# Four-layer graph network kernel: longer row and one-hot rings in passes 2 and 3, more lead, later closing steps

## The chip, the cores and the metric

One core of one Trainium2 chip runs the whole program. The metric is the device time of one execution in microseconds (us), the median of the runs. Engines are named as in the profile: PE (TensorE matmuls), PEld (its weight loads), DVE (VectorE), ACT (ScalarE), POOL (GpSimd) and SP (SyncE, which only issues DMAs here).

## The reference, cut to what matters

There are 6250 nodes with 256 features and 106250 edges, sorted by destination. Four layers follow each other, each with a residual and a layer norm. The third entry below (a two-step GCN) is what passes 2 and 3 of the kernel compute.

```python
edge_index = jnp.stack([src, dst])
x = _layernorm(x + _L0_gnn_ref(x, edge_index, ...))       # attention, gathers of x
x = _layernorm(x + _L1_gnn_ref(x, L1_gnn_W, edge_index))  # pass 1
# pass 2 is the first gcn_layer, pass 3 the second
def gcn_layer(x, row, col, w, W, b, n):
    x = x @ W
    deg = jax.ops.segment_sum(w, col, num_segments=n)
    dinv = jnp.where(deg > 0, jax.lax.rsqrt(deg), 0)
    norm = dinv[row] * w * dinv[col]
    return jax.ops.segment_sum(norm[:, None] * x[row], col, num_segments=n) + b
h = relu(gcn_layer(X, row, col, w, W1, b1, n)); h = relu(gcn_layer(h, row, col, w, W2, b2, n))
x = _layernorm(x + h)
x = _layernorm(x + _L3_gnn_ref(x, L3_gnn_W, edge_index))  # last pass
```

## The kernel before, in words

The nodes are cut into 49 blocks of 128. A segment sum into one block is done in one of two ways. In passes 2 and 3 the first 27 blocks are summed **by gathers**: 18 chunks of up to 128 edges each, so that a pass has 27 x 18 = 486 chunks. The other 22 blocks are summed **densely**: a count-and-weight matrix of the block (built in pass 1, kept in DRAM as `AW`) is loaded in pieces `aw` and multiplied with all rows of the layer (`H` in pass 2, `H4` in pass 3), 49 units of a block, 1078 units in a pass. `dense_of` (line 271) spreads the units evenly over the chunks, between two and three to a chunk.

One chunk of pass 2 or 3, numbered m over the passes and k within one, takes five steps:

- POOL (line 2697) gathers 128 rows of the table in DRAM into one of NG = 7 slots of `Gs`. It may do so once DVE's "low" step of seven chunks before has read the slot (`slot_free`, line 1060).
- ACT, `weighted_rows` (line 2088): waits for the gather, waits for TensorE's counter `s_mm` (the row matmul of chunk m - 3 has been reported done), and writes the weighted rows, rounded to fp32r, to the left half of `R[m % 3]` (line 2096).
- DVE, `onehot` (line 1610): waits for the row matmul of m - 4, writes the one-hot matrix `Mr[m % 4]` (line 1617), then waits for ACT and writes what the rounding lost to the right half of `R[m % 3]` (line 1624, "low").
- PE, `aggregate` (line 2542): issues the dense units of the chunk (line 2518), waits for "low", and multiplies `Mr[m % 4]` with `R[m % 3]` (128x512, line 2568), adding in PSUM. This raises `s_mm`; each seventh dense unit raises `s_dn`.
- SP loads the next pieces `aw` (line 2722), four buffers of seven units, each when its buffer has been read.

Every engine runs its own list in a fixed order. ACT does the rows of chunk k + 2 in turn k of its loop, DVE the one-hot and "low" of chunk k + 1. **Behind a block** that is complete at chunk k come its closing steps, which `follow_pass` (line 342) places at chunk numbers: on DVE "own" at k - 2, then "sum", "rest" and in pass 3 the layer norm (lines 1576, 1580, 1585, 1589); on ACT "relu" (line 2050) or "normalize" (line 2021); then PE "turn" (a transpose, lines 2281 and 2282), ACT "turned" one chunk later (line 1981), PE "multiply" two chunks after the turn (lines 2308 and 2309), and ACT "table" three after it (line 2013). SP (pass 2) or ACT (pass 3) stores the table's block. "own" fills one of three buffers `hb`, which is free once the turn (pass 3: the "sum") of three blocks before is done. In pass 2 all engines but SP also do the degree counts among this (DVE lines 1634 and 1637, PE line 2489).

Pass 3's gathers read the table that pass 2 stores, so POOL waits at the border for the last store. The last pass follows pass 3; its first dense work (line 2532) already runs at pass 3's end.

Of the kernel before, what the change touches and what calls it, by code (L numbers as in the profile page):

```python
# [5 lines left out]
F32 = mybir.dt.float32  # L6
F32R = mybir.dt.float32r
# [8 lines left out]
P = 128  # L16
# [51 lines left out]
KEYS_AT = 11  # L68
NAW, NR = 4, 3
FILL_C = 1  # L70
TW = 4
# [194 lines left out]
def chunks_of(p):  # L266

    return (len(GB1) if p == 1 else NB0[p]) * NC
# [73 lines left out]
def follow_pass(p):  # L342


    V_, S_, T_ = [], [], []
    for k, b in complete(p):

        rest = ("rest",) if p > 1 and b < NB0[p] else ("none",)
        if p > 1:
            V_.append((max(k - 2, 0), ("own", b)))  # L350
        if p == 2:
            for name in ("sum", *rest):
# [11 lines left out]
        else:  # L364
# [9 lines left out]
            k += 1  # L374
        T_ += [(k, ("turn", b)), (k + 2, ("multiply", b))]
        S_ += [(k + 1, ("turned", b)), (k + 3, ("table", b))]
    return by_due(V_), by_due(S_), by_due(T_)
# [431 lines left out]
def program(nc, a, out):  # L809
# [6 lines left out]
    with ExitStack() as ctx:  # L816
# [8 lines left out]
        def tiles(stack):  # L825
            return lambda n, s, d=F32: stack.enter_context(nc.sbuf_tensor(n, s, d))
# [104 lines left out]
        behind_pieces = sb("behind_pieces", [P, 136])  # L931
        W2 = sb("Wt1", [P, 2, D])
        Gs = sb("Gs", [P, NG, D + 1])
# [4 lines left out]
        Mr = [sb(f"Mr{i}", [P, P], F32R) for i in range(NM)]  # L938
        idx = sb("idx", [P, NBK, NC], U32)
        dlo, wD = sb("dlo", [P, NBK, NC]), sb("wD", [P, NBK, NC])  # L940
        iot, ident, ones = sb("iot", [P, P]), sb("ident", [P, P]), sb("ones", [P, P])
# [3 lines left out]
        W3 = sb("Wt2", [P, 2, D])  # L945
        tst = sb("tst", [P, 2, D])
        W4, W4r = W0, tst
        b1, b2 = sb("bc0", [P, D]), tst[:, 0, :]
        hb = [sb(f"hb{i}", [P, D]) for i in range(3)]
# [6 lines left out]
        turned2.close()  # L956
        R.append(sb(f"R{NR - 1}", [P, 2 * D], F32R))
        fourth = ExitStack()
        sb = tiles(fourth)
# [5 lines left out]
        big = [sb(f"big{i}", [P, 8 * (P + NBK)], BF16) for i in range(2)]  # L965
        degrees_.close()
        sb = tiles(fourth)
        G4 = sb("G4", [P, NG4, D])
# [56 lines left out]

        MOFF = {1: 0, 2: chunks_of(1), 3: chunks_of(1) + chunks_of(2), 4: chunks_of(1) + chunks_of(2) + chunks_of(3)}
        block_of = lambda p, k: GB1[k // NC] if p == 1 else k // NC

# [167 lines left out]
        def vector(e):  # L1196
# [413 lines left out]
            def onehot(p, k):  # L1610
                m = MOFF[p] + k
                b, c = block_of(p, k), k % NC
                w.wait_ge(s_mm, m - (NM1 if p == 1 else NM) + 1)
                if p == 1:
                    ins = e.tensor_scalar(M[m % NM1][:, :], iot[:, :], dlo[:, b, c:c + 1], None, ALU.is_equal)  # L1615
                else:
                    ins = e.tensor_scalar(Mr[m % NM][:, :], iot[:, :], dlo[:, b, c:c + 1], None, ALU.is_equal)  # L1617
                done(ins, ("M", m))
                if p > 1:

                    slot, _ = gather_of(pass_gather(p, k))
                    both = R[m % NR]
# [239 lines left out]
            def aggregate(p):  # L1862
                other = behind(p, 0)
                if p == 1:
                    w.wait_ge(s_wn, 6)
                end, ahead = chunks_of(p), HOT_AHEAD if p == 1 else 1
                for k in range(ahead):
# [95 lines left out]
        def scalar(e):  # L1963
# [124 lines left out]
            def weighted_rows(p, k):  # L2088

                m = MOFF[p] + k  # L2090
                slot, arrived = gather_of(pass_gather(p, k))
                w.wait_ge(s_g[slot], arrived)
                w.wait_ge(s_mm, m - NR + 1)
                if m < MOFF[2] + NR:
                    w.wait_ge(s_pj, project_at(2, NBK))
                e.activation(R[m % NR][:, 0:D], G[slot][:, 0:D], ACT.Copy, scale=wD[:, k // NC, k % NC:k % NC + 1]).then_inc(s_rw, 1)  # L2096

# [89 lines left out]
            def aggregate(p):  # L2187
                other = behind(p, 1)
                end = chunks_of(p)
                if p == 1:  # L2190
                    for i in range(2):
                        weight_columns(i)
                else:
                    for k in range(2):
                        weighted_rows(p, k)
                for k in range(end):
                    if p == 1 and k in COLUMNS_AT:
                        weight_columns(COLUMNS_AT[k])
                    if p > 1 and k + 2 < end:
                        weighted_rows(p, k + 2)  # L2200
                    for step in other[k]:
# [68 lines left out]
        def tensor(e):  # L2270
# [265 lines left out]
            def aggregate(p):  # L2536
                other = behind(p, 2)
                end = chunks_of(p)
                for k in range(end):
# [27 lines left out]
                    else:  # L2567
                        e.matmul(ps, Mr[m % NM][:, :], R[m % NR][:, :], start=c == 0, stop=c == NC - 1).then_inc(s_mm, 1)  # L2568
                    for step in other[k]:
# [148 lines left out]
        def sync(e):  # L2718
# [198 lines left out]
```

## Time and profile before

| what | value |
|---|---|
| median of 3 runs | 3711.36 us |
| the runs | 3728.65, 3711.36, 3702.01 us |
| profiled execution, first to last instruction (the span) | 3698.2 us |
| median minus this span | 13.2 us |
| TensorE busy in the span | 3173.7 us, 86% |
| GpSimd busy in the span | 2260.2 us, 61% |

The profiled execution has no time of its own listed; its span stands 13.2 us below the median, which is what lies around the first and last instruction and the difference between executions. The profile shows idle time of an engine together with what ended it ("[7.37 <-remote]": 7.37 us idle, ended by something that the profile could not name). Matmuls overlap, and the ends shown for them are modelled; their starts are recorded.

### The profile page before, as it was taken

What the parts mean: (1) busy time and instruction counts of PE and PEld (TensorE: products, weight loads), DVE (VectorE), ACT (ScalarE), POOL (GpSimd) and SP (SyncE); (2) the same over time, 40 slices, a digit from 0 to 9 for tenths busy, and PEclk for the clock granted to TensorE, in tenths of its full rate; (3) what the DMA queues carried; (4) which work ended last, traced back from release to release, by engine and by line L of the source; (5) the groups of instructions that cost most, each with busy time, mean ns of one, the idle gap of its engine ahead of it and who ended that gap; (6) DMA issues with size and microseconds to landing.
All of it is one profiled execution on the core that took longest, in us unless ns stands there. A gap on an engine that the chain in (4) does not pass through costs nothing.

```text
span 3698.2 us, 59031 instructions
## 1 busy us (share of the span) xinstructions
PE 3173.7 (86%) x18573; PEld 2529.9 (68%) x18573; DVE 2481.7 (67%) x9776; ACT 1754.3 (47%) x4617; POOL 2260.2 (61%) x2251
## 2 busy tenths in 40 slices
PE   6788788888888888789989988889898988989897
PEld 5656666666666666567777777777777776767776
DVE  5778787787778787647666666455555556566766
ACT  3556556656656656423333333334434445344444
POOL 5636566666665666556666666566666665566663
PEclk8999999999989999899999999999999999999999
DMA  5346666666666666756665655566556665756564
GB/s 178 96 153 197 189 198 182 203 193 198 201 182 205 188 193 202 254 183 184 184 183 178 184 179 181 177 188 189 182 182 192 187 192 188 246 185 208 185 198 130
DMA packets 329911, 693.24 MB, mean 187 GB/s; under 512 B 64598, under 2 KB 169500, under 8 KB 328698
## 3 DMA queue, kind: packets, MB, share of 16 engines
q1 hardware_dynamic: 215102, 392.17, 32.0%
q0 software_dynamic: 105680, 289.13, 27.3%
q10 hardware_dynamic: 8812, 8.11, 0.7%
q8 instruction: 151, 2.47, 0.3%
q14 instruction: 166, 1.36, 0.1%
HBM read 511.23 MB, written 177.95 MB: 186 GB/s over the span
## 4 chain that ended last, share of the span: by engine, by line
PE 63%; DVE 17%; issue 7%; another core or an unknown queue 5%; ACT 4%; DMA 2%; POOL 1%; ACTq 0%; SPq 0%; DVEq 0%
PE PS L2518 19%; PE PS L2623 8%; PE PS L2566 7%; PE PS L2568 6%; PE PS L2469 4%; PE PS L2442 3%; PE PS L2608 2%; PE PS L2308 2%; PE PS L2309 2%; DVE soh L1804 2%; DVE R L1624 2%; PE PS L2496 2%; DVE M L1615 1%; ACT R L2096 1%
## 5 line engine op out<-in xcount | busy, mean ns | idle before, releaser
L2697 POOL DMA_INDIRECT Gs<-T,idx x1782 | 1813.7, 1018 | 1069.8 <-issue 338.3
L2518 PE MATMUL PS<-H,aw 128*128 128x256 f32 x4312 | 1132.0, 391 | 6.7 <-DMA aw<-AW 6.2
L2518 PEld LDWEIGHTS PS<-H,aw 128*128 128x128 f32 x4312 | 831.0, 196 | 130.4 <-issue 6.9
L2096 ACT ACTIVATE R<-Gs,wD 128x256 fp32r<-128x256 f32 x972 | 483.6, 507 | 856.9 <-PE PS L2568 582.5
L1624 DVE SCALAR_TENSOR_TENSOR R<-Gs,wD,R 128x256 fp32r<-128x256 f32 x972 | 469.3, 483 | 560.7 <-ACT R L2096 299.2
L2568 PE MATMUL PS<-R,Mr 128*128 128x512 f32 x972 | 570.0, 587 | 105.3 <-DVE R L1624 83.2
L2566 PE MATMUL PS<-Gs,M 128*128 128x257 f32 x1620 | 544.6, 421 | 5.9 <-issue 3.5
L2711 POOL DMA_INDIRECT G<-T,idx x312 | 321.2, 1029 | 223.4 <-DVE R L1942 69.5
L2623 PE MATMUL PS<-HH,cr 128*128 128x512 f32 x1617 | 438.6, 399 | 3.2 <-DVE cr L1893 2.9
L2469 PEld LDWEIGHTS PS<-wdoh,soh 128*128 128x128 bf16 x3432 | 242.3, 101 | 185.9 <-issue 51.8
L2469 PE MATMUL PS<-wdoh,soh 128*128 128x128 bf16 x3432 | 290.9, 227 | 89.0 <-ACT wdoh L2151 31.2
L2623 PEld LDWEIGHTS PS<-HH,cr 128*128 128x128 f32 x1617 | 309.4, 192 | 74.3 <-DVE cr L1893 4.1
L2163 ACT CAST atp<-PS 128x512 bf16<-128x512 f32 (+1 forms) x441 | 246.7, 565 | 180.4 <-PE PS L2442 127.0
L2442 PE MATMUL PS<-soh,doh 128*128 128x256 bf16 x931 | 230.7, 285 | 107.4 <-issue 22.3
L2568 PEld LDWEIGHTS PS<-R,Mr 128*128 128x128 f32 x972 | 190.6, 196 | 172.8 <-DVE R L1624 113.4
L2566 PEld LDWEIGHTS PS<-Gs,M 128*128 128x128 f32 x1620 | 281.7, 204 | 27.5 <-issue 5.7
L1615 DVE TENSOR_SCALAR M<-iot,dlo 128x128 f32<-128x128 f32 x810 | 234.1, 292 | 76.5 <-PE PS L2566 61.5
L1617 DVE TENSOR_SCALAR Mr<-iot,dlo 128x128 fp32r<-128x128 f32 x972 | 284.0, 293 | 0.0
L1804 DVE TENSOR_SCALAR soh<-iob,clf 128x256 bf16<-128x256 bf16 x1136 | 281.8, 295 | 0.0
L2245 ACT CAST R<-G 128x256 fp32r<-128x256 f32 x312 | 124.2, 405 | 259.5 <-PE PS L2608 189.1
L2182 ACT COPY awp<-PS 128x512 f32<-128x512 f32 (+1 forms) x286 | 162.3, 569 | 146.0 <-PE PS L2469 107.8
L2151 ACT ACTIVATE wdoh<-doh,clw 128x128 bf16<-128x128 bf16 x572 | 209.6, 439 | 2.0 <-DVE M L1615 0.9
(337 smaller groups left out, 4664.4 us busy)
## 6 DMA issues: line engine op xcount, KB each, us to landing
aw<-AW SPq DMA_DIRECT2D x308, 448.0 KB
AW<-awp SPq DMA_DIRECT2D x264, 256.0 KB
AT<-atp SPq DMA_DIRECT2D x392, 128.0 KB
br<-AT SPq DMA_DIRECT2D x56, 896.0 KB
Gs<-T,idx POOLq DMA_INDIRECT x1782
AT<-atf SPq DMA_DIRECT2D x49, 256.0 KB
T<-H SPq DMA_DIRECT2D x96, 128.0 KB
cr<-AT SPq DMA_DIRECT2D x7, 1024.0 KB
```

The costliest lines, as they stand in the source:

```text
L1617: ins = e.tensor_scalar(Mr[m % NM][:, :], iot[:, :], dlo[:, b, c:c + 1], None, ALU.is_equal)
L1624: done(e.scalar_tensor_tensor(out=both[:, D:2 * D], in0=G[slot][:, 0:D], scalar=wD[:, b, c:c + 1], in1=both[:, 0:D].bitcast(F32), op0=ALU. ...
L1804: done(e.tensor_scalar(soh[n_ % NB][:, q, :], iob[:, :], clf[j][:, j0 + q:j0 + q + 1], None, ALU.is_equal), ("pairhot", n_))
L2096: e.activation(R[m % NR][:, 0:D], G[slot][:, 0:D], ACT.Copy, scale=wD[:, k // NC, k % NC:k % NC + 1]).then_inc(s_rw, 1)
L2442: ins = e.matmul(ps, d_, s_, start=j != own + 1, stop=True)
L2469: ins = e.matmul(ps[:, h * P:(h + 1) * P], soh[n_ % NB][:, q, h * P:(h + 1) * P], wdoh[n_ % NB][:, t, :, q], start=j != own + 1 and h == 0 ...
L2518: ins = e.matmul(ps, aw[n_ % NAW][:, s_ % 7, :], rows_in(p)[:, s_, :], start=s_ == 0, stop=s_ == NBK - 1)
L2566: e.matmul(ps, M[m % NM1][:, :], G[slot][:, 0:D + 1], start=c == 0, stop=c == NC - 1).then_inc(s_mm, 1)
L2568: e.matmul(ps, Mr[m % NM][:, :], R[m % NR][:, :], start=c == 0, stop=c == NC - 1).then_inc(s_mm, 1)
L2623: ins = e.matmul(bank4(s)[:, :], cr[(j + 1) % 2][:, bb, (s % 4) * P:(s % 4 + 1) * P], HH[:, :, b, :], start=b == 0, stop=b == NBK - 1)
L2697: e.indirect_dma_start(G[slot][:, 0:D], None, TAB[p][0:N, :], bass.IndirectOffsetOnAxis(ap=idx[:, block_of(p, k), k % NC:k % NC + 1], axis ...
L2711: e.indirect_dma_start(G4[:, n_ % NG4, :], None, TAB[4][0:N, :], bass.IndirectOffsetOnAxis(ap=idx4[:, s_ // 2, s_ % 2, c:c + 1], axis=0)). ...
```

## The change: what it does

- The ring `R` of passes 2 and 3 has 5 buffers in pass 2 and 7 in pass 3 (before: 3). The ring `Mr` of one-hots has 8 and 10 (before: 4). `ring` gives for each chunk its buffer and the count that `s_mm` must have reached.
- ACT writes rows 3 chunks ahead in pass 2 and 4 in pass 3 (before: 2). DVE works 2 and 3 chunks ahead (before: 1).
- The closing steps of a block begin 3 chunks later in pass 2 and 4 in pass 3 ("own" stays where it was). "turn" comes a further 3 or 4 chunks later, "turned" 4 or 5 behind it (before 1), "multiply" 2 or 3 behind that (before 1), "table" 4 or 5 behind that (before 1), and the turn or product of a block comes no earlier than "turned" or "table" of the block before. The shifts shrink to nothing towards chunk 462 (`CLOSE_BY`). SP's place for a store is 3 or 4 chunks later, too.
- The new buffers lie in memory that is free by then: over `Wt1`, `tst`, the last 22 blocks' part of `idx` and `wD`, and the degree tiles. The second bias moves from `tst` to the unused part of `dlo`. ACT's first row of pass 2 waits for the stores of the table; its first of pass 3 waits for the last degree matmul.

```diff
+RINGS, HOTS = {2: 5, 3: 7}, {2: 8, 3: 10}
+ROWS_BEFORE, HOTS_BEFORE, SUMS_LATER = {2: 3, 3: 4}, {1: HOT_AHEAD, 2: 2, 3: 3}, {2: 3, 3: 4}
+CLOSE_BY = 24
...
+    free = 0, 0
     for k, b in complete(p):
...
         if p > 1:
+            room = max(0, (chunks_of(p) - CLOSE_BY - k) // 2)
             V_.append((max(k - 2, 0), ("own", b)))
+            k += min(SUMS_LATER[p], room)
...
-        T_ += [(k, ("turn", b)), (k + 2, ("multiply", b))]
-        S_ += [(k + 1, ("turned", b)), (k + 3, ("table", b))]
+        there, back = (0, 0) if p == 1 else (min(x, room) for x in (ROWS_BEFORE[p], SUMS_LATER[p]))
+        turn = max(k + there, free[0])
+        turned = turn + 1 + back
+        product = max(turned + 1 + there // 2, free[1])
+        table = product + 1 + back
+        if p > 1:
+            free = turned, table
+        T_ += [(turn, ("turn", b)), (product, ("multiply", b))]
+        S_ += [(turned, ("turned", b)), (table, ("table", b))]
...
+        def ring(sizes):
+            used_by, out = {}, {}
+            for p in (2, 3):
+                for k in range(chunks_of(p)):
+                    m, i = MOFF[p] + k, k % sizes[p]
+                    out[m] = i, used_by.get(i, MOFF[2] - 1) + 1
+                    used_by[i] = m
+            return out
...
-                w.wait_ge(s_mm, m - (NM1 if p == 1 else NM) + 1)
...
+                    hot, read = HOTS_AT[m]
+                    w.wait_ge(s_mm, read)
+                    ins = e.tensor_scalar(Mr[hot][:, :], iot[:, :], dlo[:, b, c:c + 1], None, ALU.is_equal)
...
-                end, ahead = chunks_of(p), HOT_AHEAD if p == 1 else 1
+                end, ahead = chunks_of(p), HOTS_BEFORE[p]
...
-                w.wait_ge(s_mm, m - NR + 1)
-                if m < MOFF[2] + NR:
+                at_, read = ROWS_AT[m]
+                w.wait_ge(s_mm, read)
+                if m == MOFF[2]:
                     w.wait_ge(s_pj, project_at(2, NBK))
+                    w.wait_ge(s_t2[0], 16 * ((NBK + 1) // 2))
+                    w.wait_ge(s_t2[1], 16 * (NBK // 2))
+                if m == MOFF[3]:
+                    w.wait_ge(s_dgs, NDEG)
...
-                    if p > 1 and k + 2 < end:
-                        weighted_rows(p, k + 2)
+                    if p > 1 and k + ROWS_BEFORE[p] < end:
+                        weighted_rows(p, k + ROWS_BEFORE[p])
...
-                return [(d + 1, (store, p + 1, s_[1])) for d, s_ in FOLLOW[p][1] if s_[0] == "table"]
+                return [(d + 1 + (ROWS_BEFORE[p] if p > 1 else 0), (store, p + 1, s_[1])) for d, s_ in FOLLOW[p][1] if s_[0] == "table"]
```

## Rows read from the trace of the kernel before

**Rows 1.** The page: span and busy times.
```profile
span 3698.2 us, 59031 instructions
PE 3173.7 (86%) x18573; PEld 2529.9 (68%) x18573; DVE 2481.7 (67%) x9776; ACT 1754.3 (47%) x4617; POOL 2260.2 (61%) x2251
```

**Rows 2.** Busy time by stage: pass 2, border, pass 3, its end, what follows.
```profile
core 0: us, PE busy (x) PEld busy (x) DVE busy (x) ACT busy (x) POOL busy (x), PEclk, DMA share, GB/s
1593.20:2362.20 769.00, 691.71 (x3723) 560.37 (x3721) 485.76 (x1654) 290.12 (x628) 504.25 (x478) 0.97 0.60 181
2362.20:2377.60 15.40, 14.37 (x68) 12.09 (x66) 2.75 (x7) 2.79 (x6) 6.16 (x7) 1.00 0.60 191
2377.60:3098.00 720.40, 645.29 (x2791) 536.14 (x2790) 403.88 (x1456) 290.31 (x644) 463.59 (x463) 0.95 0.60 185
3098.00:3133.00 35.00, 25.36 (x88) 17.46 (x87) 28.99 (x102) 24.04 (x70) 19.84 (x18) 0.85 0.56 190
3133.00:3170.00 37.00, 36.29 (x160) 29.49 (x158) 11.33 (x34) 6.62 (x18) 9.97 (x10) 1.00 0.94 353
```

**Rows 3.** Waits between 1594 and 3098 us: total us, times, longest us.
```profile
ACT R L2096 <- PE PS L2568: 575.9, 542, 7.7
...
ACT R L2096 <- remote: 115.2, 54, 7.4
...
PE PS L2568 <- DVE R L1624: 80.2, 58, 4.8
...
PE PS L2308 <- issue: 17.9, 7, 4.1
PE PS L2281 <- ACT X L2021: 11.0, 6, 4.2
PE PS L2281 <- issue: 11.0, 8, 3.0
```

**Rows 4.** Timeline of pass 2, 2238 to 2250 us (start, us, engine, line).
```profile
2237.99 0.58 PE L2568 MATMUL PS<-R,Mr 128*128 128x512 f32 x1
...
2239.52 0.58 PE L2568 MATMUL PS<-R,Mr 128*128 128x512 f32 x1
...
2240.61 0.58 PE L2568 MATMUL PS<-R,Mr 128*128 128x512 f32 x1
...
2241.03 1.02 PE L2518 MATMUL PS<-H,aw 128*128 128x256 f32 x4
...
2245.76 1.31 ACT L2096 ACTIVATE R<-Gs,wD 128x256 fp32r<-128x256 f32 x3 [7.37 <-remote]
2246.30 0.48 DVE L1624 SCALAR_TENSOR_TENSOR R<-Gs,wD,R 128x256 fp32r<-128x256 f32 x1 [7.20 <-ACT R L2096]
...
2246.84 0.80 PE L2568 MATMUL PS<-R,Mr 128*128 128x512 f32 x1 [4.79 <-DVE R L1624]
...
2247.82 2.05 PE L2518 MATMUL PS<-H,aw 128*128 128x256 f32 x4
...
2249.98 1.35 POOL L2697 DMA_INDIRECT Gs<-T,idx  x1 [0.30 <-issue]
```

**Rows 5.** Busy time before, in and after that stall; columns as in rows 2.
```profile
2226.00:2242.00 16.00, 16.00 (x88) 13.29 (x86) 10.14 (x35) 5.62 (x12) 12.34 (x13) 1.00 0.63 198
2242.00:2246.80 4.80, 0.05 (x1) 0.00 (x0) 0.50 (x2) 1.04 (x3) 1.40 (x2) 0.86 0.29 81
2246.80:2252.00 5.20, 5.16 (x19) 4.04 (x20) 4.52 (x16) 1.59 (x4) 3.96 (x4) 0.50 0.46 138
```

**Rows 6.** Line 2697 between 1600 and 3090 us; POOL's groups in pass 2, in pass 3.
```profile
L2697 POOL DMA_INDIRECT Gs<-T,idx x942: 943/949/2282, 1599.3 to 3089.5; - x189
...
L2697 POOL DMA_INDIRECT Gs<-T,idx x477 | 502.7, 1054 | 253.1 <-issue 88.9 <-DVE Mr L1617 80.2 <-DVE R L1624 48.8
...
L2697 POOL DMA_INDIRECT Gs<-T,idx x463 | 464.5, 1003 | 257.1 <-issue 84.2 <-DVE Mr L1617 79.2 <-DVE R L1624 43.4
```

**Rows 7.** Timeline of the border between pass 2 and pass 3.
```profile
2367.69 0.32 SPq L2722 DMA_DIRECT2D T<-H  x1
...
2369.61 0.95 POOL L2697 DMA_INDIRECT Gs<-T,idx  x1 [14.65 <-DMA T<-H]
...
2377.56 0.58 PE L2568 MATMUL PS<-R,Mr 128*128 128x512 f32 x1
```

More of the change, by code:

```diff
@@ L931, in program @@
         behind_pieces = sb("behind_pieces", [P, 136])
-        W2 = sb("Wt1", [P, 2, D])
+        second = ExitStack()
+        W2 = tiles(second)("Wt1", [P, 2, D])
+        second.close()
+        R3 = sb("R3", [P, 2 * D], F32R)
         Gs = sb("Gs", [P, NG, D + 1])
@@ L938, in program, with hots_behind @@
         Mr = [sb(f"Mr{i}", [P, P], F32R) for i in range(NM)]
-        idx = sb("idx", [P, NBK, NC], U32)
-        dlo, wD = sb("dlo", [P, NBK, NC]), sb("wD", [P, NBK, NC])
+        def hots_behind(name, dtype):
+            edges = ExitStack()
+            t_ = tiles(edges)(name, [P, NBK, NC], dtype)
+            edges.close()
+            sb(f"{name}_kept", [P, NBW, NC], dtype)
+            Mr.extend([sb(f"Mr{len(Mr) + i}", [P, P], F32R) for i in range(3)])
+            sb(f"{name}_rest", [P, 16])
+            return t_
+        idx = hots_behind("idx", U32)
+        dlo = sb("dlo", [P, NBK, NC])
+        wD = hots_behind("wD", F32)
         iot, ident, ones = sb("iot", [P, P]), sb("ident", [P, P]), sb("ones", [P, P])
@@ L945, in program @@
         W3 = sb("Wt2", [P, 2, D])
-        tst = sb("tst", [P, 2, D])
+        staged = ExitStack()
+        tst = tiles(staged)("tst", [P, 2, D])
+        staged.close()
+        R4 = sb("R4", [P, 2 * D], F32R)
         W4, W4r = W0, tst
-        b1, b2 = sb("bc0", [P, D]), tst[:, 0, :]
+        b1 = sb("bc0", [P, D])
+        unused = lambda t_: t_[:, NBW:NBK, :].rearrange("p b c -> p (b c)")
+        b2 = unused(dlo)[:, 0:D]
         hb = [sb(f"hb{i}", [P, D]) for i in range(3)]
@@ L957, in program @@
         R.append(sb(f"R{NR - 1}", [P, 2 * D], F32R))
+        R += [R3, R4]
         fourth = ExitStack()
@@ L966, in program @@
         degrees_.close()
+        third = ExitStack()
+        R += [tiles(third)(f"R{i}", [P, 2 * D], F32R) for i in range(len(R), RINGS[3])]
+        third.close()
         sb = tiles(fourth)
@@ L1026, in program @@
         MOFF = {1: 0, 2: chunks_of(1), 3: chunks_of(1) + chunks_of(2), 4: chunks_of(1) + chunks_of(2) + chunks_of(3)}
+        def ring(sizes):
[6 more added lines that the diff above has]
+            return out
+        ROWS_AT, HOTS_AT = ring(RINGS), ring(HOTS)
         block_of = lambda p, k: GB1[k // NC] if p == 1 else k // NC
@@ L1612, in onehot @@
                 b, c = block_of(p, k), k % NC
-                w.wait_ge(s_mm, m - (NM1 if p == 1 else NM) + 1)
                 if p == 1:
+                    w.wait_ge(s_mm, m - NM1 + 1)
                     ins = e.tensor_scalar(M[m % NM1][:, :], iot[:, :], dlo[:, b, c:c + 1], None, ALU.is_equal)
                 else:
-                    ins = e.tensor_scalar(Mr[m % NM][:, :], iot[:, :], dlo[:, b, c:c + 1], None, ALU.is_equal)
+                    hot, read = HOTS_AT[m]
+                    w.wait_ge(s_mm, read)
+                    ins = e.tensor_scalar(Mr[hot][:, :], iot[:, :], dlo[:, b, c:c + 1], None, ALU.is_equal)
                 done(ins, ("M", m))
@@ L1621, in onehot @@
                     slot, _ = gather_of(pass_gather(p, k))
-                    both = R[m % NR]
+                    both = R[ROWS_AT[m][0]]
                     w.wait_ge(s_rw, m - MOFF[2] + 1)
@@ L2092, in weighted_rows @@
                 w.wait_ge(s_g[slot], arrived)
-                w.wait_ge(s_mm, m - NR + 1)
-                if m < MOFF[2] + NR:
+                at_, read = ROWS_AT[m]
+                w.wait_ge(s_mm, read)
+                if m == MOFF[2]:
                     w.wait_ge(s_pj, project_at(2, NBK))
-                e.activation(R[m % NR][:, 0:D], G[slot][:, 0:D], ACT.Copy, scale=wD[:, k // NC, k % NC:k % NC + 1]).then_inc(s_rw, 1)
+                    w.wait_ge(s_t2[0], 16 * ((NBK + 1) // 2))
+                    w.wait_ge(s_t2[1], 16 * (NBK // 2))
+                if m == MOFF[3]:
+                    w.wait_ge(s_dgs, NDEG)
+                e.activation(R[at_][:, 0:D], G[slot][:, 0:D], ACT.Copy, scale=wD[:, k // NC, k % NC:k % NC + 1]).then_inc(s_rw, 1)
             def high(q):
@@ L2193, in aggregate @@
                 else:
-                    for k in range(2):
+                    for k in range(ROWS_BEFORE[p]):
                         weighted_rows(p, k)
@@ L2567, in aggregate @@
                     else:
-                        e.matmul(ps, Mr[m % NM][:, :], R[m % NR][:, :], start=c == 0, stop=c == NC - 1).then_inc(s_mm, 1)
+                        e.matmul(ps, Mr[HOTS_AT[m][0]][:, :], R[ROWS_AT[m][0]][:, :], start=c == 0, stop=c == NC - 1).then_inc(s_mm, 1)
                     for step in other[k]:
```

## The prediction

> **What bounds the kernel now.** I read the page first, then the busy time by stage, the waits of the two passes, and one stretch of the timeline. The page says that TensorE is busy for 86% of the span and GpSimd for 61% [rows 1]; that is an average over stages, and the change touches only passes 2 and 3, 1593 to 3133 us. There the stages show TensorE idle for 769.0 - 691.7 = 77.3 us in pass 2 and for 720.4 - 645.3 = 75.1 us in pass 3 up to 3098 us, 152.4 us together [rows 2]. The granted clock was 0.97 and 0.95 there, so 0.03 x 769 + 0.05 x 720.4 = 59 us more went to matmuls at 1.2 instead of 2.4 GHz. All that is open to the change is thus 152 + 59 = 211 us; the rest is TensorE's own work: 769 - 77 - 23 = 669 us for 486 chunks, 1.376 us each, and in pass 3 609 us for some 463 chunks (the gathers of that stretch count them), 1.316 us each.
>
> What stops TensorE is seen in the waits: 58 times it stood for DVE's second half of the rows, 80 us in total and never over 4.8 us; next come products and transposes of the closing steps. DVE waits for ACT, and ACT most of all for the row matmul that frees a buffer: 576 us in 542 waits, and 115 us in 54 waits whose releaser has no name [rows 3]. Most of the 576 us are harmless, a full ring in front of a busy TensorE. The timeline shows the harmful ones. The row matmuls went out at 2237.99, 2239.52 and 2240.61 us, the dense ones behind them at 2241.03. ACT needed the first of these three to be reported before it could refill its buffer, and got the word after 7.37 us idle; then it wrote three rows within 1.31 us, so all three reports had come almost at once [rows 4]. Had TensorE itself been late, the reports would have come a chunk apart. So TensorE had done the work, the report was late, and a ring of three ran dry: from its last dense work it stood until 2246.84 us. I see no cause for the late report, only that it recurs and that gathers and loads were not behind it: POOL went on issuing until its seven slots were full. After the stall the clock was 0.50 for the 5.2 us shown, against 1.00 before it [rows 5], and four dense matmuls took 2.05 instead of 1.02 us [rows 4].
>
> **The rings.** From the report to the next row matmul it takes 2246.84 - 2245.76 = 1.08 us (ACT, then DVE) [rows 4]. From the first unreported row at 2237.99 TensorE can go on for as many chunks as the ring is deep. With three: 7.77 + 1.08 - 3 x 1.376 = 4.7 us of standstill, and 4.79 are shown. With five in pass 2: 8.85 - 6.9 = 2.0 us; with seven in pass 3: 8.85 - 9.2, none. This was about the longest event, since ACT's longest wait is 7.7 us [rows 3]. A stall under 2 x 1.376 = 2.75 us vanishes in pass 2, one under 4 x 1.316 = 5.3 us in pass 3. The mean of TensorE's 58 waits is 1.4 us. I leave 10 us of the idle time in pass 2 and 5 us in pass 3; the bounds are 0 and all 152. The clock follows: 6 of 59 us stay, bounds 0 and 59. The buffers cost nothing: no instruction is added but a few waits at the start of each pass, for stores that the first gather awaits anyway (its own wait was 14.65 us, for the store [rows 7]) and for degree work that ended before.
>
> **The lead of ACT and DVE** alone would gain nothing from a deeper ring if an earlier instruction in their fixed lists waited for TensorE. It is what the two constants and the later closing steps are for. DVE's "sum" waits for TensorE's chunk k and now stands where DVE has prepared k + 5 (pass 3: k + 7), the depth of the ring. "turned" stands 4 or 5 chunks behind the transpose and the product 6 or 8 behind it, before 2; so 6 x 1.376 = 8.3 us are covered, more than the longest late report. The waits of lines 2281 and 2308 [rows 3] are in the 152 us and go with it. "own" keeps its place: its buffer was last used by a block three completions before, at least 22 chunks earlier by the kernel's schedule, and a turn now at about k + 9 to k + 20 still precedes it in TensorE's list. In pass 3 that buffer is freed by "sum". Cost nothing, bounds 0 and 5 us.
>
> **What is late next: the gathers.** A gather takes 1.054 us on POOL in pass 2 and 1.003 in pass 3, and 0.30 us lie between two [rows 4, 6]. That is 1.354 and 1.303 us a chunk, against TensorE's 1.376 and 1.316. TensorE still sets the pace, but by only 1.6% and 1.0%. Two machines with nearly the same pace and a dozen buffers between them disturb each other: now POOL is idle over a third of the time and catches up; then it hardly can. No row shows this state. Below, it costs nothing; above, if all of TensorE's time waited on a gather pace 10% worse, 0.1 x 1278 = 128 us. I take 2% of 669 + 609 = 26 us, near the low end, since the gather itself is the measured row.
>
> **The ends.** The border of 15.4 us [rows 2] stays: the last store went out at 2367.69 and its landing released POOL at 2369.61 [rows 7]. SP's stores now stand 3 places later, behind loads of pass 3, but the last store was behind them before. At pass 3's end some tables come later, by up to 18 chunks; there TensorE has 37 us of dense work of the last pass, 36.3 of it busy [rows 2], which hides them. I take 3 us for both; bounds 0, and 18 x 1.376 = 25 us if nothing hides them.
>
> **Sum.** 211 - 15 - 6 - 26 - 3 = 161 us saved. On the profiled execution: 3698.2 - 161 = 3537 us span; with the 13.2 us between span and median, 3711.4 - 161 = 3550 us.
>
> **A rule that speaks against it.** Gathers took 0.949 us at the median and up to 2.28 us [rows 6], and it is in pass 2, with DVE's denser work, that the mean is higher. The Trainium skill, page "SBUF — State Buffer", section "SBUF: two separate sides", says that VectorE and GpSimd share a port pair under an exclusive lock, and that GpSimd cannot write its descriptors while VectorE holds it. By that rule a DVE that works in less time delays each gather more often; that is the first rival.
>
> **Rivals.**
> - *POOL sets the pace* (chance 0.15). The excess over 0.949 us doubles, as gathers have less quiet time: 1.159 and 1.057, plus 0.30 is 1.459 and 1.357 us a chunk; 486 x 1.459 + 463 x 1.357 = 1337 us instead of 1489, and 2% coupling and the ends cost 30: 122 us saved, 3589 us. For: only 1% between the two paces. Against: the median is at the minimum, so most gathers are undelayed.
> - *The lead is lost again* (0.12). At each of 98 closings ACT or DVE waits in its list until TensorE catches up, and a late report within it strikes as before. Half of 211 us returns, less 16 for coupling and ends: 90 saved, 3622 us. For: three closings at adjacent chunks push each other. Against: the spacing above.
> - *TensorE itself stops* and the records of its starts mislead (0.09). Then only the waits of the closing steps go, rows with 17.9 + 11.0 + 11.0 us [rows 3] and smaller ones; some 25 us: 3686 us. Against: three reports within 1.31 us.
> - *Slower* (0.04): DVE and ACT, no longer held back, run in bursts and stretch the gathers behind them to what is seen right after the stall, 1.35 us [rows 4]. It decides from a mean of 769 / 486 - 0.30 = 1.28 us on, where POOL's pace is the present one of pass 2. At 1.35: 1.65 x (486 + 463) - 1489 = 77 us more, 3788 us.
>
> **Chances and range.** The forecast has 0.60; its own range is 3505 to 3595 (all of the 211 us gone but the ends, to double the coupling and triple the leftover). To hold 8 of 10 the range takes in the first two rivals: 3495 to 3645 us. This kernel's measurement tells about 1% from no change, 37 us. Faster by more: forecast and first two rivals, 0.87. Within 1%: the third, 0.09. Slower: 0.04.
>
> **What would show it.** Right, if TensorE's idle time in the two passes falls from 152 to under 50 us, the clock there is 0.98 or more, ACT's longest waits for line 2568 remain near 7 us while TensorE's waits for line 1624 shrink, and POOL's mean stays under 1.08 us at a pitch near 1.38. The first rival shows as POOL back to back with a mean over 1.1 us and TensorE's waits passing through DVE and ACT to a gather. The second shows as waits of ACT for lines 2282 or 2309, or DVE's for `s_dn`. The third leaves idle time at row matmuls as it was. I am wrong in the main step if TensorE stays idle for over 100 us there.

## The result, and the profile after

| what | before | changed |
|---|---|---|
| median of 16 runs each, same chip | 3708.35 us | 3684.94 us |
| ratio, 95% interval | | 0.9929 (0.991 to 0.9948) |
| profiled execution, span | 3698.2 us | 3684.6 us |

The change makes the kernel 0.7% faster, 23 us between the medians, where I forecast 161; the two profiled executions are 13.6 us apart. All ratios of this document are of executions in the fast state: of all executions only one, of the run e8, was in the slow one (4280.14 us at a granted clock of 0.65, its neighbours 0.99). The busy time by stage of the changed kernel answers to [rows 2]: pass 2, border, pass 3, its end (columns as there: us, busy us by engine, granted clock, DMA share, GB/s).

```profile
1594.50:2361.00 766.50, 697.35 (x3701) 566.56 (x3700) 480.49 (x1651) 272.89 (x625) 506.28 (x478) 0.95 0.60 181
2361.00:2378.00 17.00, 15.97 (x74) 13.45 (x73) 2.02 (x6) 2.25 (x5) 3.79 (x4) 1.00 0.45 131
2378.00:3090.00 712.00, 641.84 (x2781) 533.54 (x2780) 394.12 (x1449) 271.59 (x640) 458.19 (x464) 0.95 0.61 188
3090.00:3124.00 34.00, 27.61 (x107) 19.70 (x106) 30.24 (x110) 24.38 (x70) 18.67 (x18) 0.95 0.58 193
```

TensorE is still idle for 69.2 + 70.2 = 139 us of the two passes, before 152 us [rows 2], and its clock did not rise (0.95 and 0.95, before 0.97 and 0.95). The waits between 1594 and 3098 us (total us, times, longest us) say that it is another idle time than before:

```profile
ACT R L2153 <- PE PS L2625: 455.2, 261, 5.7
...
ACT R L2153 <- remote: 200.7, 61, 8.0
...
PE PS L2575 <- issue: 41.6, 65, 1.7
PE PS L2365 <- ACT H L2065: 37.1, 13, 5.7
...
PE PS L2338 <- ACT xT L2033: 13.6, 6, 5.2
...
PE PS L2625 <- DVE R L1676: 9.1, 6, 5.2
...
PE PS L2625 <- issue: 8.5, 15, 1.6
```

The wait that the ring was meant for, row matmul for DVE's second half, fell from 80.2 us in 58 times [rows 3] to 9.1 us in 6. ACT still waits up to 8.0 us for a report, as before. What came in its place are two things: product (L2365) and turn (L2338) wait for ACT, and dense matmuls (L2575) stand for "issue", that is, for nothing that the profile names. Added up from the same view of either kernel, TensorE's idle time went from 96 to 18 us at row matmuls, from 56 to 69 us at turns and products, and from 1 to 51 us at dense and degree matmuls. One late report in full, pass 2 of the changed kernel (start, us, engine, line):

```profile
2077.36 0.51 ACT L2153 ACTIVATE R<-Gs,wD 128x256 fp32r<-128x256 f32 x1 [1.37 <-DMA Gs<-T,idx]
...
2079.55 0.58 PE L2625 MATMUL PS<-R,Mr 128*128 128x512 f32 x1
...
2080.64 0.58 PE L2625 MATMUL PS<-R,Mr 128*128 128x512 f32 x1
...
2081.06 0.47 PE L2546 MATMUL PS<-big 128*128 128x49 bf16 x8
...
2082.70 1.02 PE L2575 MATMUL PS<-H,aw 128*128 128x256 f32 x4 [1.16 <-issue]
...
2083.50 0.51 ACT L2153 ACTIVATE R<-Gs,wD 128x256 fp32r<-128x256 f32 x1 [5.63 <-remote]
...
2084.85 0.48 PE L2575 MATMUL PS<-H,aw 128*128 128x256 f32 x1 [0.33 <-issue]
...
2085.56 0.48 PE L2575 MATMUL PS<-H,aw 128*128 128x256 f32 x1 [0.23 <-issue]
...
2086.27 0.55 PE L2575 MATMUL PS<-H,aw 128*128 128x256 f32 x1 [0.24 <-issue]
...
2087.06 0.51 ACT L2153 ACTIVATE R<-Gs,wD 128x256 fp32r<-128x256 f32 x1 [3.06 <-remote]
```

ACT hears nothing for 5.63 us. Before, TensorE would have stood at an empty ring; now it has rows and goes on, until about 2081.5 us. There it stands for 1.16 us before a dense matmul, which needs no row. The report that comes by 2083.50 is followed by another 3.06 us of silence, and in these the dense matmuls start only one per 0.71 us (2084.85, 2085.56, 2086.27), where four had taken 1.02 us. The ring of five has moved the stop, not removed it.

POOL has hardly changed. Its groups in pass 2 and in pass 3 give means of 1.058 and 0.987 us, against 1.054 and 1.003 us [rows 6]:

```profile
L2754 POOL DMA_INDIRECT Gs<-T,idx x477 | 504.8, 1058 | 247.9 <-issue 84.6 <-DVE Mr L1669 79.2 <-DVE R L1676 38.4
```

```profile
L2754 POOL DMA_INDIRECT Gs<-T,idx x464 | 458.2, 987 | 251.2 <-issue 102.7 <-DVE Mr L1669 59.0 <-DVE R L1676 50.3
```

### The profile page after: what moved, and what is told of

The parts are those of the page before. It is cut to its first block, busy times and chain, and to the rows that moved or that the text cites. A ratio compares the mean times of both kernels' runs of the same rounds, so it can differ in the third digit from the quotient of the medians.

```text
span 3684.6 us, 58999 instructions
## 1 busy us (share of the span) xinstructions
PE 3190.8 (87%) x18573; PEld 2544.8 (69%) x18573; DVE 2472.4 (67%) x9776; ACT 1722.7 (47%) x4617; POOL 2253.3 (61%) x2251
## 4 chain that ended last, share of the span: by engine, by line
PE 69%; DVE 15%; issue 6%; another core or an unknown queue 4%; ACT 3%; DMA 2%; POOL 1%; ACTq 0%; SPq 0%; DVEq 0%
PE PS L2575 24%; PE PS L2680 9%; PE PS L2623 7%; PE PS L2625 6%; PE PS L2526 4%; PE PS L2499 3%; PE PS L2365 3%; PE PS L2665 3%; PE PS L2366 2%; DVE soh L1856 2%; PE PS L2553 2%; DVE M L1665 1%; DVE OHP L1834 1%; DVE doh L1854 1%
## 5 line engine op out<-in xcount | busy, mean ns | idle before, releaser
L2575 PE MATMUL PS<-H,aw 128*128 128x256 f32 x4312 | 1149.9, 393 | 49.7 <-issue 41.6
L2575 PEld LDWEIGHTS PS<-H,aw 128*128 128x128 f32 x4312 | 831.8, 197 | 197.5 <-issue 73.8
L2153 ACT ACTIVATE R<-Gs,wD 128x256 fp32r<-128x256 f32 x972 | 466.7, 504 | 933.1 <-PE PS L2625 455.2
L1665 DVE TENSOR_SCALAR M<-iot,dlo 128x128 f32<-128x128 f32 x810 | 232.7, 289 | 88.2 <-PE PS L2623 70.2
```

The lines of the kernel that those rows point to most:

```text
L2153: e.activation(R[at_][:, 0:D], G[slot][:, 0:D], ACT.Copy, scale=wD[:, k // NC, k % NC:k % NC + 1]).then_inc(s_rw, 1)
L2575: ins = e.matmul(ps, aw[n_ % NAW][:, s_ % 7, :], rows_in(p)[:, s_, :], start=s_ == 0, stop=s_ == NBK - 1)
```

## The experiments

Two theories at first. **A**: TensorE itself is held while its reports are late, so a deeper ring only moves its idle time. **B**: the ring works, but the lead is lost at the closing steps, since `free` lets a block's turn fall on the very chunk at which the block before is turned, and its product on that of the table before. After the first four runs a third: **C**, the late reports belong to the chip. Each batch of runs below had a chip of its own, so "the chip" stands for the chip and for whatever else went on around it at that time; the runs can't tell these apart.

### Parts of the change, and wider closings

The first run keeps the rings and the lead alone (`SUMS_LATER = {2: 0, 3: 0}` and the second line below), the second the closing steps alone (rings 3 and 4, leads 2 and 1, `there` still 3 and 4), the third and fourth widen the closings of the changed kernel:

```diff
 # e1, the rings alone
-        there, back = (0, 0) if p == 1 else (min(x, room) for x in (ROWS_BEFORE[p], SUMS_LATER[p]))
+        there, back = 0, 0
 # e3 and e4
-            free = turned, table
+            free = turned + there, table + there
 # e4 only
-        product = max(turned + 1 + there // 2, free[1])
+        product = max(turned + 1 + there, free[1])
```

> The rings of 5 and 7, the one-hot rings and the lead of 3 and 4 chunks alone; the closing steps stand where they stood before. Theory A (TensorE itself is held while its reports are late, so a deeper ring moves its idle time and removes little): 3685 to 3705 us, idle of TensorE in passes 2 and 3 about 140 us, of it under 20 us in waits of row matmuls for DVE. Theory B (the deep ring works, and what is lost now is the lead at the closings, where turn and product of one block fall on the chunk at which the block before it is turned and evicted): the closings stand closer still, so waits of L2338 and L2365 for ACT of over 60 us, and 3700 to 3720 us.

> The later and wider closing steps alone, with the rings of 3 and 4 and the leads of 2 and 1 of the kernel before. Theory A: the late reports still empty the ring of three, so TensorE waits about 80 us for DVE's rows as before, and 3695 to 3712 us. Theory B: the same for the rows, and the waits of the closings as in the changed kernel (some 50 us), 3700 to 3715 us. If this alone gives 3685 us, both theories are wrong about which part brought the 0.7%.

> The changed kernel, but a block's turn comes 'there' chunks (3 or 4) behind the chunk of the transposed copy of the block before, and its product so many behind that block's table. Theory A: the waits of turns and products for ACT (13.6 and 37.1 us) shrink, but the idle time reappears as issue time at dense matmuls and row matmuls: 3675 to 3690 us. Theory B: those waits fall under 15 us and their idle time and the slow clock behind it go, 50 to 60 us: 3625 to 3640 us.

> As the run with the margin between blocks, and the product of a block also stands 3 or 4 instead of 1 or 2 chunks behind its own transposed copy. Theory A: no better than 3670 to 3690 us. Theory B: a further few us below the run with the margin, 3620 to 3635 us, with no wait of L2365 for ACT over 5 us in total.

All four ran on a chip on which the kernel before takes 3179.28 us, not 3708. Ratios to it: 0.9996 (0.9982 to 1.0009), 1.0006 (0.9994 to 1.0018), 0.9987 (0.9976 to 0.9999), 0.9983 (0.9971 to 0.9995). No edit moves the time by more than 0.2%, and ACT's longest wait for a row matmul was 2.2 us in the first of them. My expectations had all been written for a chip on which reports come late, and missed. What follows is only that this chip has nothing for the change to hide.

### The two kernels once more, and TensorE cut loose from the rows

The third run lets the row matmul of passes 2 and 3 read one fixed one-hot and one fixed tile of rows, so TensorE waits for no gather, ACT or DVE; the fourth also leaves the gathers, rows and one-hots of the two passes out, but for the first chunk.

```diff
 # e7 (and e15): the rows are still prepared, in rings of their own
-                    w.wait_ge(s_v, at["M", m] if p == 1 else at["low", m])
+                    w.wait_ge(s_v, at["M", m] if p == 1 else at["low", m if k == end - 1 else MOFF[2]])
...
-                        e.matmul(ps, Mr[HOTS_AT[m][0]][:, :], R[ROWS_AT[m][0]][:, :], ...
+                        e.matmul(ps, Mr[HOTS[2]][:, :], R[RINGS[2]][:, :], ...
 # e8 (and e16), POOL's list; ACT's and DVE's likewise
+                    if p == 1 or (p == 2 and k == 0):
                         e.indirect_dma_start(G[slot][:, 0:D], None, TAB[p][0:N, :], ...
```

> The changed kernel itself once more, because the chip of the last four runs needed 3179 us for the kernel before instead of 3708 us and showed no wait of ACT for a row matmul above 2.2 us. New theory C: the late reports of TensorE belong to the chip, not to the kernel. Where the kernel before takes about 3180 us, no row-matmul wait is over 3 us, TensorE's wait for rows is under 10 us in either kernel, and the changed kernel is within 0.2% of it. Where it takes about 3700 us, the late reports are there again, and the changed kernel is 0.5 to 0.9% faster. Theory A and B (the causes lie in the kernel's own order) have late reports at either speed.

> The kernel before once more, for its profile on the chip of these runs. Theory C: at about 3180 us, its waits of TensorE for DVE's second half of the rows are under 10 us in all, against 80 us at 3698 us, and the granted clock is 0.98 to 0.99; at about 3700 us they are 80 us again. Theories A and B: some 80 us at either speed.

> The changed kernel, but in passes 2 and 3 the row matmul reads one fixed one-hot and one fixed tile of rows, so it waits for no gather, ACT or DVE; the rows and one-hots are still prepared beside it, into rings of 4 and 7. Its sums are not those of the reference. At about 3180 us for the kernel before: TensorE has nothing to gain, within 15 us of it. At about 3700 us, theory A (TensorE is held with its reports): passes 2 and 3 keep over 100 us of idle time, mostly issue, and the time is 3650 to 3690 us. Theory B: idle time under 50 us and 3600 us or less.

> As the run with fixed tiles, and in passes 2 and 3 the gathers, ACT's rows and DVE's one-hots and second halves are left out but for the first chunk; dense work, closings, tables, loads and stores stay. Its output is not the reference's. At about 3180 us for the kernel before: TensorE's own work sets the end, 3140 to 3180 us. At about 3700 us, theory A with reports that are late whatever the other engines do: as the run with fixed tiles, within 20 us. If the late reports come from the gathers' load, they are gone in these two passes: idle time of TensorE under 30 us there and 3500 to 3560 us.

Another chip, on which the kernel before takes 3180.04 us. The changed kernel took 3181.60 us, ratio 1.0006 (0.9995 to 1.0016); TensorE on fixed tiles 1.0005 (0.9989 to 1.0021); without the other engines' work 3157.74 us, 0.9918 (0.99 to 0.9936). C had the times right in all four. It had also said that ACT would wait for no row matmul for over 3 us; the longest such wait was 4.0 us in the kernel before. The kernel before on this chip, pass 2 and pass 3 by stage:

```profile
1349.20:2004.10 654.90, 653.28 (x3721) 550.44 (x3720) 490.67 (x1654) 293.71 (x628) 486.40 (x478) 1.00 0.71 213
...
2019.50:2657.20 637.70, 625.42 (x2877) 536.06 (x2876) 439.27 (x1558) 316.32 (x714) 480.33 (x480) 0.99 0.72 219
```

and its waits of TensorE for rows between 1349 and 2650 us:

```profile
PE PS L2568 <- DVE R L1624: 6.1, 8, 1.6
```

The same program needs 1308.0 us for its two passes and the border, where the first chip needed 3133.0 - 1593.2 = 1540 us [rows 2], with TensorE idle for 14 us instead of 162 (the 152 and 9.6 more at the end of pass 3 [rows 2]). The changed kernel needs 1308.5 us here.

### A late report, imitated

Where no report is late by itself, one can be imitated, as far as the rows go: ACT is held, while all of TensorE's reports stay on time. In 37 chunks of each pass ACT writes the rows eight times, seeing the end of each before the next, and only the last is reported. The edit went into the kernel before, the changed one, the rings alone (as e1) and the widest closings (as e4).

```diff
+                for _ in range(7 if k % 13 == 6 else 0):
+                    e.activation(R[m % NR][:, 0:D], G[slot][:, 0:D], ACT.Copy, scale=...).then_inc(s_late, 1)
+                    held[0] += 1
+                    w.wait_ge(s_late, held[0])
                 e.activation(R[m % NR][:, 0:D], G[slot][:, 0:D], ACT.Copy, scale=...).then_inc(s_rw, 1)
```

> A late report is imitated where none comes by itself: in the kernel before, ACT writes the rows of one chunk in thirteen of passes 2 and 3 eight times over, each time after it has seen the end of the last, which holds them back by some 4 to 5 us (75 chunks). If the ring arithmetic of the prediction holds, a ring of three lets TensorE go on for about 2 chunks' time of slack and it stands for 2 to 3.5 us each time: 150 to 260 us above this chip's kernel before. If the rows were not what TensorE waits for, under 30 us.

> The same hold in the changed kernel. Ring arithmetic: rings of 5 and 7 give 2.75 and 5.3 us more, so the hold vanishes but for a few us: 0 to 40 us above this chip's kernel before, so 120 to 250 us less than the kernel before with the same hold. If the rings didn't help even here (a wait elsewhere in the lists of ACT and DVE), it is over 100 us.

> The same hold with the rings and the lead alone, closing steps where they were before. If the later closing steps are what keeps the lead, this is 20 to 100 us slower than the changed kernel with the hold, with waits of TensorE for ACT at turns and products; if the rings do it alone, within 10 us of it.

> The same hold with wider margins between the closing steps of two blocks. If the changed kernel's closings still cost the lead, this is 10 to 40 us faster than the changed kernel with the hold; if not, within 5 us of it.

The hold in the timeline of the kernel before (e9): seven extra writes take 3.75 us.

```profile
1374.85 3.75 ACT L2098 ACTIVATE R<-Gs,wD 128x256 fp32r<-128x256 f32 x7
```

| with the hold | median, us | above this chip's 3182.52 us |
|---|---|---|
| kernel before (e9) | 3329.18 | 147 |
| rings alone (e11) | 3256.45 | 74 |
| changed kernel (e10) | 3237.87 | 55 |
| widest closings (e12) | 3220.27 | 38 |

The intervals of the four ratios (1.0455 to 1.0504, 1.0199 to 1.0252, 1.0158 to 1.0192, 1.0113 to 1.0146) don't touch. A hold of 3.8 us costs the kernel before 147 / 74 = 2.0 us each time, a little under what I expected. The rings take half of it away, the later closing steps 19 us more, wider closings 18 us more. The changed kernel was to lose 40 us at most and loses 55, and its later closing steps were to bring 20 at least; the gain of the wider closings lay within my 10 to 40 us. The waits of TensorE show how. The kernel before (1352 to 2806 us):

```profile
PE PS L2573 <- DVE R L1625: 86.1, 69, 2.8
```

The changed kernel (1361.6 to 2724.5 us):

```profile
PE PS L2370 <- ACT H L2066: 16.4, 9, 3.0
PE PS L2630 <- DVE R L1677: 15.3, 19, 1.9
PE PS L2343 <- ACT xT L2034: 14.4, 7, 4.7
```

The widest closings (1357 to 2701.5 us):

```profile
PE PS L2630 <- DVE R L1677: 37.3, 41, 2.7
...
PE PS L2370 <- ACT xT L2034: 0.5, 1, 0.5
```

In the changed kernel product and turn wait for ACT, as they did in its own profile; a margin between two blocks' closings takes these waits away, and some of the time comes back as waits for rows. So B is a real loss of this change wherever ACT falls behind.

### The late reports themselves

The next chip had them. All four kernels ran beside the kernel before, 3657.44 us.

> The changed kernel on another chip yet. If the kernel before takes about 3700 us here: 0.5 to 0.9% faster, TensorE idle for some 140 us in the two passes. If about 3180 us: within 0.2%, no row-matmul wait of ACT over 4 us.

> The wider margins between closings. At about 3700 us for the kernel before: if what the late reports cost the changed kernel is mostly lost at the closings (theory B), 3620 to 3650 us; if TensorE is held itself (theory A), 3670 to 3690 us. At about 3180 us: 3170 to 3180 us as before.

> Row matmuls on fixed tiles (their sums are not the reference's), the rest as it is. At about 3700 us for the kernel before: theory A leaves over 100 us of TensorE's idle time in the two passes, theory B under 50 us. At about 3180 us: within 0.2%.

> The same, and the gathers, rows and one-hots of passes 2 and 3 left out but for the first chunk. At about 3700 us for the kernel before: within 20 us of the run with fixed tiles if the reports are late whatever the others do; 3500 to 3560 us if they come from the gathers' load. At about 3180 us: 3155 to 3162 us as before.

| kernel | median, us | ratio, 95% | TensorE idle, pass 2 + 3 |
|---|---|---|---|
| changed (e13) | 3632.83 | 0.9933 (0.991 to 0.9956) | 62.4 + 67.7 = 130 us |
| widest closings (e14) | 3625.03 | 0.9921 (0.9882 to 0.9959) | 59.6 + 62.9 = 122 us |
| fixed tiles (e15) | 3682.76 | 1.0078 (1.0048 to 1.0108) | 69.2 + 88.3 = 158 us |
| no gathers, rows, one-hots (e16) | 3423.30 | 0.9351 (0.9309 to 0.9392) | 0.0 + 1.6 = 2 us |

The changed kernel repeats its 0.7%. With the widest closings the waits for ACT are gone, and the time has moved to issue. The changed kernel (e13, 1570.2 to 3075 us):

```profile
PE PS L2575 <- issue: 58.6, 100, 1.7
PE PS L2365 <- ACT H L2065: 15.9, 10, 4.0
PE PS L2365 <- issue: 15.1, 7, 4.6
PE PS L2625 <- issue: 11.1, 22, 1.7
```

The widest closings (e14, 1571.4 to 3073.5 us):

```profile
PE PS L2575 <- issue: 69.2, 108, 1.7
PE PS L2546 <- issue: 18.3, 29, 1.2
PE PS L2625 <- issue: 18.3, 30, 2.7
```

8 us between the medians is less than the intervals can tell. The time itself, 3625 us, lies in the range that I had given to B, but that was meant for a kernel before of 3700 us: as ratios, B had 0.978 to 0.986 and A 0.992 to 0.997, and 0.9921 was measured. B therefore holds little of the idle time on such a chip, and A most of it. The run on fixed tiles shows A bare. Passes 2 and 3 by stage (e15):

```profile
1570.00:2336.60 766.60, 697.36 (x3723) 569.28 (x3721) 475.98 (x1651) 271.21 (x622) 506.20 (x478) 0.95 0.61 182
...
2351.90:3114.10 762.20, 673.88 (x2874) 553.93 (x2872) 416.76 (x1553) 297.09 (x707) 483.88 (x480) 0.93 0.60 184
```

No row matmul waits for rows here, and TensorE is idle as before. Its timeline early in pass 3 shows how it is held:

```profile
2369.16 0.58 PE L2577 MATMUL PS<-H,aw 128*128 128x256 f32 x1 [0.82 <-issue]
2371.97 0.58 PE L2577 MATMUL PS<-H,aw 128*128 128x256 f32 x1 [2.23 <-issue]
2374.76 0.58 PE L2627 MATMUL PS<-R,Mr 128*128 128x512 f32 x1 [2.21 <-issue]
2377.56 0.59 PE L2577 MATMUL PS<-H,aw 128*128 128x256 f32 x1 [2.21 <-issue]
2380.36 0.59 PE L2577 MATMUL PS<-H,aw 128*128 128x256 f32 x1 [2.21 <-issue]
```

One matmul per 2.80 us, four times running, dense ones and the fixed row matmul alike. By the semaphore records of the same trace, no counter that TensorE raises was updated between 2368.45 and 2388.91 us. So TensorE is held while its reports are late, with all its data there, and no ring can reach this. It isn't a gap in the records either: they hold as many matmuls as on the chip without late reports (3723 and 2874 in the two passes, 3721 and 2877 there). That it is slower than the kernel before, by 0.8%, although it waits for less, I can't explain.

And without gathers, rows and one-hots it is gone, on the same chip (e16):

```profile
1577.20:2229.30 652.10, 652.10 (x3722) 550.84 (x3721) 186.65 (x689) 59.19 (x145) 1.52 (x1) 1.00 0.41 117
...
2244.70:2864.30 619.60, 617.98 (x2873) 533.84 (x2872) 144.38 (x588) 82.90 (x224) 0.00 (x0) 1.00 0.41 123
```

1287.1 us with the border, and 1287.0 us in the same run on the chip without late reports (e8). So what holds TensorE needs both: this chip (or its state at that time), and the load of the left-out work. For this outcome I had expected 3500 to 3560 us beside 3700, a ratio of 0.946 to 0.962; it is 0.9351, so more went with the left-out work than I had put on it.

I also went through the counters that TensorE raises, for stretches of over 2.2 us without an update in which at least two matmuls that raise one had ended (by their modelled ends). In e15 there were 175 between the first and the last row matmul of the two passes. In e16 there was none there, and 141 outside, where its gathers are as before. The kernel before had 308 in the whole program and the changed one 324, on the chip of e5 to e8 at most one.

### Which part of the load

The first run keeps only the gathers (paced by TensorE's report, seven ahead), the second only the work of ACT and DVE.

```diff
 # e17: as e8, and every gather is issued
+                    else:
+                        w.wait_ge(s_mm, MOFF[p] + k - NG + 1)
+                        w.wait_ge(s_g[slot], landed - 16)
 # e17, TensorE's list: its last row matmul waits for the last seven gathers
+                    if p == 3 and k == end - 1:
+                        for j in range(NG):
+                            w.wait_ge(s_g[gather_of(pass_gather(p, k - j))[0]], gather_of(pass_gather(p, k - j))[1])
 # e18: as e7, no gather but the first; ACT and DVE also wait for TensorE
-                w.wait_ge(s_mm, MOFF[2])
+                w.wait_ge(s_mm, max(read, MOFF[2]))
```

> Row matmuls on fixed tiles; in passes 2 and 3 the gathers are issued as ever, seven ahead of TensorE's report, but ACT's rows and DVE's one-hots and second halves are left out but for the first chunk (output not the reference's). Where the kernel before takes about 3650 to 3700 us: if the gathers are what makes TensorE's reports late, the two passes keep over 100 us of idle time and the kernel is within 40 us of the kernel before; if the work of ACT and DVE is, it is near the run without all of them, 6.5% under the kernel before. Where it takes about 3180 us: 3155 to 3165 us, and nothing is told apart.

> The complement: fixed tiles, no gathers in passes 2 and 3 but the first, ACT's rows and DVE's one-hots and second halves all there, on whatever the slots hold (output not the reference's). Where the kernel before takes about 3650 to 3700 us: 6.5% under it if the gathers are the cause, within 40 us of it if ACT's and DVE's work is; each about half if both add up. Where it takes about 3180 us: 3155 to 3180 us.

The chip was one without late reports (3180.16 us), so the question stays open. The gathers alone took 3173.51 us, ratio 0.9979 (0.9968 to 0.9989), the rows alone 3197.30 us, 1.0054 (1.0037 to 1.007). Both lie above what I expected (3155 to 3165 and 3155 to 3180), and in both the edit has a part in it.

With the gathers alone the two passes and the border took 1294.6 us, without them (e8, another such chip) 1287.0. Of these 7.6 us one wait takes nearly all, the one that the edit gave to TensorE's last row matmul of pass 3:

```profile
PE PS L2628 <- DMA Gs<-T,idx: 6.8, 1, 6.8
```

In pass 2, which has no such wait, 652.0 us stand against 652.1: the gathers cost TensorE nothing there.

With the rows alone they took 1325.7 us, and TensorE was idle for 29.1 us of pass 3. Nearly all of this are waits for ACT at turns and products, up to 3.5 us each (pass 3 of e18: total us, times, longest us):

```profile
PE PS L2341 <- ACT xT L2033: 13.9, 12, 3.4
PE PS L2368 <- ACT H L2065: 11.6, 11, 1.1
PE PS L2368 <- ACT xT L2033: 3.5, 1, 3.5
```

By its lists, ACT writes 4 chunks ahead in pass 3 of this edit, into a ring of 4. So in turn k of its list it waits for the row matmul of chunk k itself before it gets to the closing steps, and has no lead left. In pass 2, 3 ahead with the same ring, such waits come to about 1 us. With a ring no deeper than the lead the closings waited here without any late report.

## Why the prediction was wrong, point by point

- **What is open to the change** was sized well. I put TensorE's own work at 669 us for pass 2 and 609 for most of pass 3, and 211 us as lost. On a chip without late reports the passes and the border take 1308 us instead of 1540, 232 us less.
- **The step that failed** is "So TensorE had done the work, the report was late, and a ring of three ran dry". The second half is true for the moment shown. But I drew from it that TensorE could go on as long as it had rows, and it can't: in the changed kernel it is slowed to one matmul per 0.71 us with rows at hand, and on fixed tiles to one per 2.80 us. TensorE stayed idle for 139 us, over the 100 us that I had named as the mark of being wrong in the main step. The 190 us that the rings were to free (152 - 15 of idle time and 59 - 6 of slow clock) were thus mostly never theirs: the idle time fell by 13 us and the clock did not rise.
- **The ring arithmetic** was right about the wait it described: TensorE's waits for rows went from 80 to 9 us, and against an imitated late row the rings save 73 us of 147. It priced one cause and took it for all.
- **The lead at the closings** I costed at nothing, bounds 0 and 5 us, in the belief that the spacing behind a chunk was enough. I did not look at the spacing between the closings of two blocks, which `free` puts at zero. Its waits were 37.1 and 13.6 us. That is the rival "the lead is lost again"; its mechanism is there (18 us of the imitated 55), its price of 71 us is not: on the late chip 8 us, and within the intervals.
- **The rival "TensorE itself stops"** named 3686 us, and 3684.94 came. That it came so near is luck. Its saving was to come from the waits at turns and products, but these grew from 56 to 69 us; and the rows named for it, 17.9 + 11.0 + 11.0, add up to 39.9 us and not to the "some 25" that 3686 was made of. Half its mechanism is right, TensorE does stop; its mark, idle time at row matmuls as it was, was wrong, and so was the reason I gave against it. Three reports within 1.31 us [rows 4] say that the first two were late, not that TensorE was free to go on.
- **"Gathers and loads were not behind it"** I read from POOL going on issuing. That tells that POOL wasn't stopped, not that its traffic does no harm; without the gathers, rows and one-hots not one late report was left in the two passes. Which of the three does the harm is open.
- **The coupling of the two paces**, 26 us: not seen. On a chip without late reports all gathers cost TensorE under 1 us (7.6 less the 6.8 of one added wait), and POOL as pace-setter, the first rival, had nothing behind it: the means of a gather stayed at 1.058 and 0.987 us. The Trainium skill, page "SBUF — State Buffer", section "SBUF: two separate sides", says that VectorE and GpSimd share a port pair under an exclusive lock. In its direction the traces agree: without DVE's and ACT's work on the chunks a gather took 0.957 and 0.953 us in the mean (e17, pass 2 and pass 3), with it 1.017 and 1.002 us (e6, also without late reports). That it takes longer where DVE does the same work in less time they don't show: in e6, with passes 15% shorter, the means are under the 1.054 and 1.003 us of [rows 6]. In the changed kernel itself the case never arose, as its passes were hardly shorter.
- **The range of the forecast**: doubling the 26 us and tripling the 21 us of leftover, as I wrote, gives 3550 + 26 + 42 = 3618 us and not 3595. The result lies outside either, and outside the 3645 us of the wide range.
- **The ends**, 3 us: the border between the row matmuls of the two passes takes 15.4 us in both kernels, and from the last row matmul to the end of the span it is 3698.2 - 3133.0 = 565.2 us before and 3684.6 - 3123.7 = 560.9 us after. Neither end costs anything.

Open: which part of the load holds TensorE, and by what. One candidate can't be tried here. Each execution of the tables above has a span, so each was recorded. The Trainium skill, page "NOTIFIC — the notification-queue block", section "7.1 Overflow: three behaviours, one of which stalls the engine", says that the block which writes the profiler's records holds its producers back rather than lose a record inside it. A gather makes many records (those left out in e16 are 46,600 of 329,900 DMA packets). That would fit a hold that comes with the gathers, if it is they; why it should differ by chip it doesn't say. No run here tests it, and if it is so, the late reports cost only executions that are recorded.

## What to carry to other kernels

When an engine hears late from another, ask whether the late one is free to go on, and look for the answer in a place where it has all its data; the chain of waits names only the buffer that ran out first. An imitated delay on a chip without the trouble prices a ring and its neighbours cleanly (here 147, 74, 55, 38 us), and shows which fixed place in the lists gives way next. On both chips that ran both, the version with the widest closings was not slower than the changed kernel (3625 to 3633 us on the late one, within the intervals), and it was the faster of the two against the imitated delay (3220 to 3238 us). And an edit made for an experiment can have a cost of its own: look for its waits by name before a difference is read as the effect.

## What the runs showed of the hardware that I had not expected

The same program took 3657 to 3708 us on two chips and 3179 to 3183 us on four others, 15 to 17% apart, with nearly the same durations of single instructions: a row matmul took 585 to 589 ns in the mean on the slower (578 there without the load), 576 to 581 on the others, ACT's rows 502 to 508 ns on either. On the two slower ones TensorE's reports come in bursts after silences that held ACT for up to 8.0 us in the changed kernel and 9.2 us in e15, and TensorE's matmuls then start at steps of 0.71 or 2.80 us. This change, which hides waiting, is worth 0.7% on the one kind of chip and nothing on the other.
